# A third mixture of experts computed on its chosen pairs, and rows stationary in the routed first product

## The reference

```python
def _L2_ffn_ref(x, gate_w, fc1_w, fc1_b, geglu_mult, fc2_w, fc2_b, s_fc1_w, ...):
    E, TOPK = (15, 3)                              # F = 256, shared FS = 512
    scores = jax.nn.softmax(xt @ gate_w.T, axis=-1)
    topk_w, topk_idx = jax.lax.top_k(scores, TOPK)
    topk_w = topk_w / (jnp.sum(topk_w, axis=-1, keepdims=True) + 1e-20)
    h = jnp.einsum('td,efd->etf', xt, fc1_w) + fc1_b[:, None, :]
    xh, g = (h[..., :F], h[..., F:])
    a = jax.nn.gelu(g, approximate=False) * xh * geglu_mult[:, None, :]
    yexp = jnp.einsum('etf,edf->etd', a, fc2_w) + fc2_b[:, None, :]
    y = jnp.einsum('etd,te->td', yexp, comb)       # + the shared expert, 512 wide

def _L3_ffn_ref(u, g_shared, W1_s, b1_s, W2_s, b2_s, g_routed, W1_r, b1_r, W2_r, b2_r, centroids):
    E_R, E_S, K = (8, 2, 2)                        # H = 1024
    # shared experts on every token, then per token the K of 8 chosen by sigmoid(u @ centroids)
```

## Time and profile before

| | |
|---|---|
| median of 3 runs | 2613.74 us (2607.96 to 2623.17) |
| profiled execution | 2616.16 us, its span 2614.3 us |
| granted clock of TensorE, mean | 0.886 |
| TensorE busy (matmul) | 2166.2 us, 83% of the span |
| VectorE busy | 1535.2 us, 59% |
| ScalarE busy | 1121.6 us, 43% |
| GpSimd busy | 586.0 us, 22% |
| HBM read and written | 154.11 MB and 18.38 MB |

### The profile page before, as it was taken

How to read it: one execution, slowest core, us unless ns; L and a number is a source line. 1 busy time by engine, 2 the same in 40 slices (tenths; PEclk the granted TensorE clock), 3 DMA queues, 4 the chain that set the end, 5 groups by cost and what they waited for, 6 DMA issues and landing times. The chain is left out here.

```text
span 2614.3 us, 42273 instructions
## 1 busy us (share of the span) xinstructions
PE 2166.2 (83%) x14834; PEld 1685.9 (64%) x14834; DVE 1535.2 (59%) x3631; ACT 1121.6 (43%) x3143; POOL 586.0 (22%) x725
## 2 busy tenths in 40 slices
PE   5799674668999976869978868989996999798893
PEld 3566441226777754559956538879995566598883
DVE  4566648996556553556555554545554556556865
ACT  5566344452444433533311444523332366455652
POOL 0200017992000010010022420000003222213555
PEclk9899787899999986669977979979997899697987
DMA  3000012210000003314310014322210000245762
GB/s 110 9 2 2 33 67 76 64 63 33 1 1 1 1 31 115 111 62 165 116 41 0 5 31 122 92 95 92 92 43 35 5 8 4 92 155 174 228 212 87
DMA packets 58247, 174.92 MB, mean 67 GB/s; under 512 B 18327, under 2 KB 28155, under 8 KB 56008
## 3 DMA queue, kind: packets, MB, share of 16 engines
q1 hardware_dynamic: 56012, 169.23, 20.1%
q0 software_dynamic: 2048, 3.29, 0.4%
HBM read 154.11 MB, written 18.38 MB: 66 GB/s over the span
## 5 line engine op out<-in xcount | busy, mean ns | idle before, releaser
L2410 PE MATMUL ps<-l1a_zc,tables_sb 128*128 128x400 f32 x256 | 108.8, 558 | 95.2 <-POOL l1a_zc L2339 60.3
L2410 PEld LDWEIGHTS ps<-l1a_zc,tables_sb 128*128 128x128 f32 x256 | 47.3, 202 | 156.6 <-POOL l1a_zc L2339 88.3
L1912 ACT ACTIVATE l1x_probs<-ps,l1x_nmax 100x361 f32<-100x361 f32 x128 | 70.7, 558 | 164.5 <-DVE l1x_nmax L1987 164.5
L2350 POOL TENSOR_TENSOR l1a_dbx<-l1a_dx,l1a_rows 128x400 f32<-128x400 f32 x128 | 130.5, 1059 | 7.0 <-DMA l1a_rows<-l1a_rows_spilled 4.9
L2363 ACT ACTIVATE ps<-l1a_delta,weights 128x400 f32<-128x400 f32 x128 | 76.5, 598 | 81.1 <-DVE ps L2393 53.1
L1026 ACT ACTIVATE l3x_probs<-l3x_s_sb,l3x_nmax 100x361 f32<-100x361 f32 x128 | 75.3, 589 | 70.4 <-DVE l3x_nmax L1115 66.4
L1024 ACT ACTIVATE l0x_probs<-ps,l0x_nmax 100x361 f32<-100x361 f32 x128 | 70.7, 557 | 65.0 <-DVE l0x_nmax L1122 56.8
L3024 PE MATMUL ps<-l3f_routed_x_high,l3f_routed_w_low 128*128 128x128 f32 x320 | 95.5, 298 | 3.5 <-DVE l3f_routed_w_low L3088 1.7
L3025 PE MATMUL ps<-l3f_routed_x_high,l3f_routed_w_high 128*128 128x128 f32 x320 | 95.3, 298 | 0.0
L3026 PE MATMUL ps<-l3f_routed_x_low,l3f_routed_w_high 128*128 128x128 f32 x320 | 95.2, 298 | 0.0
L2602 PE MATMUL ps<-l2f_x_high,l2f_w_high 128*128 128x400 f32 x272 | 95.0, 349 | 0.0
(11 more groups left out here) (714 smaller groups left out, 6754.5 us busy)
## 6 DMA issues: line engine op xcount, KB each, us to landing
ctxT<-l_ffn_units SPq DMA_DIRECT2D x20, 1026.0 KB, 5.7
l3f_expert<-l_ffn_units SPq DMA_DIRECT2D x20, 1026.0 KB, 5.5
l2x_a_taps<-l2x_taps_spread SPq DMA_DIRECT2D x8, 1912.5 KB
l2f_landing<-l_ffn_units SPq DMA_DIRECT2D x17, 771.0 KB, 6.0
l1a_rows<-l1a_rows_spilled SPq DMA_DIRECT2D x32, 400.0 KB, 3.5
l1f_gates<-l1f_gates SPq DMA_DIRECT2D x16, 800.0 KB, 4.1
l1f_positions<-l1f_staged SPq DMA_DIRECT2D x16, 621.9 KB
l1f_landing<-l_ffn_units SPq DMA_DIRECT2D x16, 512.0 KB, 3.5
```

The source lines that it names most:

```text
L2350: pool.tensor_tensor(dbx[:, n % BUFS, :], dx[:, j, m, :], rows[:, g % RING, 0, :], ALU.mult).then_inc(s.dbx_ready, 1)
L2410: pe.matmul(y_bank(m), st.ident, zc[:, n % DONE, :], start=(i == 0), stop=(i == NS - 1)).then_inc(s.sum_done, 1)
```

## The change

The third mixture takes the form of the fourth. Its two shared units stay dense, and its 15 experts run on chosen pairs: 3 a token, 33 tiles of 128 rows, one unit a tile (a unit now is the whole expert: 512 first columns, 256 hidden). Only one of the four slots is filled ahead during the shared units, because of memory (`early=1`); the other three are allocated at the start of the routed part.

In the routed part of both mixtures the first product is turned round: the rows (`x_high`, `x_low`) are stationary and the weights move, 512 columns in one matmul. The hidden values then come out with rows on partitions. The bias is one more matmul: a 64-row pick of the tile's expert (`pick`, made on GpSimd from `mine`) against the bias rows, high parts in rows 0 to 31 and low parts in rows 32 to 63. Gelu is one instruction instead of four; TensorE turns the hidden values (`turn_hidden`), and ScalarE and VectorE cut them from PSUM. The second product runs two units behind the first instead of one. The high parts of the first weights are made on ScalarE (`cut_first`) instead of VectorE. Rows have six slots (`ROW_SLOTS`), in `XT`, instead of two. In the tail a batch's power (`rstd_pool`) stands three batches behind its gathers, instead of behind all of them. At the start of the program the first pack is issued ahead of `XT`, the first stage starts without waiting for `X`, and `ctxT` is loaded after it.

```diff
 class Routes:
     SLOTS = 4
...
-        self.landing = [spare[:, i * size:(i + 1) * size].rearrange("p (q c) -> p q c", q=2) for i in range(2)]
-        self.landing += [sb(f"expert{i}", [P, 2, unit_cols])[:] for i in range(2, self.SLOTS)]
+        self.landing = [spare[:, i * q * c:(i + 1) * q * c].rearrange("p (q c) -> p q c", q=q) for i in range(lent)]
+        self.early, self.slot_shape = early, [P, q, c]
+        self.landing += [sb(f"expert{i}", self.slot_shape)[:] for i in range(lent, early)]
...
     def sync_first_loads(self, sp):
-        for u in range(self.SLOTS):
+        for u in range(self.early):
             self.sync_load(sp, u)
...
 def routed_experts(nc, st, routes, kind, bias, gain=None):
...
             @block.sync
             def _(sp):
                 def load_rows(i):
-                    after(sp, s.x_turned, i - 1)
...
+                    after(sp, s.x_turned, i - ROW_SLOTS + 1)
...
+                for u in range(routes.early, R):
+                    routes.sync_load(sp, u)
                 sp.wait_ge(routes.scattered, 16 * B * routes.top)
-                load_rows(0)
-                load_rows(1)
+                for i in range(ROW_SLOTS):
+                    load_rows(i)
                 for u in range(U):
                     if u + R < U:
                         sp.wait_ge(s.w1_split, u + 1)
                         sp.wait_ge(s.w2_split, u + 1)
-                        sp.wait_ge(s.gelu_done, 4 * (u + 1))
+                        if geglu:
+                            sp.wait_ge(s.h_split, u + 1)
                         routes.sync_load(sp, u + R)
...
+                    if u % H == H - 1 and u // H + ROW_SLOTS < N:
+                        load_rows(u // H + ROW_SLOTS)
+                    done = u // H - 1
+                    if u % H == 0 and done >= 0:
+                        sp.wait_ge(s.y_copied, done + 1)
+                        sp.dma_start(routes.results[done * P:(done + 1) * P, :], y_rows[done % 2][:]).then_inc(routes.stored[done % 2], 16)
...
                 def first(u):
...
-                    after(pe, s.gelu_done, 4 * (u - 1))
-                    for j in range(4):
-                        out = h_bank(u, j)
-                        for k in range(KT):
-                            lo, hi = w1(w_low, u, j // 2, k, j % 2), w1(w_high, u, j // 2, k, j % 2)
-                            pe.matmul(out, r(lo), r(x_high[i % 2][:, k, :]), start=(k == 0), stop=False)
-                            pe.matmul(out, r(hi), r(x_high[i % 2][:, k, :]), start=False, stop=False)
-                            last = pe.matmul(out, r(hi), r(x_low[i % 2][:, k, :]), start=False, stop=(k == KT - 1))
...
+                    pe.wait_ge(s.pick_ready, i + 1)
+                    after(pe, s.hidden_done, u - 1)
+                    pe.matmul(h_bank(u), r(pick[i % 2][:]), r(bias_parts[:, h * 512:(h + 1) * 512]), start=True, stop=False)
+                    for k in range(KT):
+                        hi, lo = r(x_high[i % 2][:, k, :]), r(x_low[i % 2][:, k, :])
+                        pe.matmul(h_bank(u), hi, r(w1(w_low, u, k)), start=False, stop=False)
+                        pe.matmul(h_bank(u), hi, r(w1(w_high, u, k)), start=False, stop=False)
+                        last = pe.matmul(h_bank(u), lo, r(w1(w_high, u, k)), start=False, stop=(k == KT - 1))
...
+                def turn_hidden(u):
+                    pe.wait_ge(s.hidden_done, u + 1)
+                    after(pe, s.h_split, u - 1)
+                    for j in range(J):
+                        last = pe.transpose(turned_bank(u)[:, j, :], hidden[u % 2][:, j, :], st.ident)
...
-                for u in range(U):
...
-                    first(u)
-                    if u:
-                        second(u - 1)
-                second(U - 1)
...
+                for u in range(U + 2):
+                    if u < U:
+                        if turns_at(u) is not None:
+                            turn_rows(turns_at(u))
+                        first(u)
+                    if 1 <= u <= U:
+                        turn_hidden(u - 1)
+                    if u >= 2:
+                        second(u - 2)
...
             @block.vector
...
-                for u in range(U):
+                for u in range(U + 3):
                     if u + 1 < U:
                         split_first(u + 1)
...
+                    if u < U and turns_at(u) is not None:
+                        split_rows(turns_at(u))
+                    if u >= 3 and (u - 3) % H == H - 1:
+                        copy_results((u - 3) // H)
+                    if u < U and geglu:
+                        product(u)
+                    if 1 <= u <= U:
+                        split_hidden(u - 1)
...
 def l2_ffn(nc, st, dram):
...
-        experts(nc, st, "l2f", "geglu", E + 2, landing, gate,
-                lambda i, sl: i * 2 + sl, [(0, xf)], st.w["f8b2"])
-        experts_tail(nc, st, "l2f")
+        experts(nc, st, "l2f", "geglu", 2, landing, gate, lambda i, sl: E + sl, [(0, xf)], st.w["f8b2"], routes)
+        routed_experts(nc, st, routes, "geglu", st.w["f8b1"])
+        routed_tail(nc, st, routes)
```

More of the change, by code:

```diff
@@ L2818, with __init__ @@
 ROW_TILES = -(-TOK // P)
+GATHER_LAG = 3
+ROW_SLOTS = 6
 class Routes:
     SLOTS = 4
-    def __init__(self, nc, ctx, st, name, experts, top, units, first_unit, unit_cols, constants, spare):
+    def __init__(self, nc, ctx, st, turn, name, experts, top, units, first_unit, halves, unit_cols, constants, who, source, spare=None, early=SLOTS):
         def sb(n, shape, dt=F32):
@@ L2957, in sb @@
             return ctx.enter_context(nc.sbuf_tensor(f"{name}_routed_{n}", shape, dt))
-        w_high, w_low = [sb(f"w_high{i}", [P, 2, offb]) for i in range(2)], [sb(f"w_low{i}", [P, 2, offb]) for i in range(2)]
-        x_rows = [sb(f"x_rows{i}", [P, D]) for i in range(2)]
+        landing = routes.landing
+        landing += [sb(f"expert{i}", routes.slot_shape)[:] for i in range(routes.early, R)]
+        w_high, w_low = [sb(f"w_high{i}", [P, Q, offb]) for i in range(2)], [sb(f"w_low{i}", [P, Q, offb]) for i in range(2)]
@@ L2964, in routed_experts @@
+        hidden = [sb(f"hidden{i}", [P, J, P]) for i in range(2)]
+        h_high, h_low = [sb(f"h_high{i}", [P, J, P]) for i in range(2)], [sb(f"h_low{i}", [P, J, P]) for i in range(2)]
         y_rows = [sb(f"y_rows{i}", [P, D]) for i in range(2)]
-        sems = ["rows_loaded0", "rows_loaded1", "x_turned", "x_cut", "x_split", "w1_cut", "w1_split", "w2_cut", "w2_split",
-                "h_ready", "gelu_done", "h_cut", "h_split", "second_done", "y_copied"]
+        pick = [sb(f"pick{i}", [64, P]) for i in range(2)]
@@ L2977, in after @@
                     eng.wait_ge(sem, value)
-            def weights_here(eng, u):
-                eng.wait_ge(routes.loaded[u % R], 16 * (u // R + 1))
             @block.sync
@@ new lines, in _ @@
+                cut_first(0)
+                cut_rows(0)
+                for u in range(U + 2):
+                    if u + 1 < U:
+                        cut_first(u + 1)
+                    if u < U:
+                        if turns_at(u) is not None:
+                            cut_rows(turns_at(u))
+                        raise_hidden(u)
+                    if 1 <= u <= U:
+                        cut_hidden(u - 1)
+                    if u < U:
+                        cut_second(u)
@@ L3118, in _ @@
                 for u in range(U):
+                    i = u // H
+                    if u % H == 0:
+                        after(pool, s.h_ready, H * (i - 1))
+                        pool.tensor_copy(r(pick[i % 2][:]), routes.mine[:, i:i + 1].to_broadcast([64, P])).then_inc(s.pick_ready, 1)
                     pool.wait_ge(s.w2_cut, u + 1)
@@ L3131, in routed_tail @@
         y = st.yT[:].rearrange("p m (b t) -> p m b t", b=B)
-        with stage_sems(nc, NORM_SEMS + [f"gathered{j}" for j in range(B)] + ["shares_added"]) as s, nc.Block(no_gpsimd_drain=True) as block:
-            gathered = [s.gathered0, s.gathered1, s.gathered2, s.gathered3, s.gathered4, s.gathered5, s.gathered6, s.gathered7]
+        with stage_sems(nc, NORM_SEMS + ["shares_added"]) as s, nc.Block(no_gpsimd_drain=True) as block:
+            gathered = routes.gathered
             @block.gpsimd
```

222 lines of the change are left out of this document (135 added, 87 removed).

## The result

The changed kernel took 2841.49 us (median of 4 runs, 2829.16 to 2846.57) against 2618.45 for the one before (4 runs): ratio 1.0848, interval 1.0793 to 1.0904. It is 8.5% slower, where 2597 was predicted.

The account below looks back on a forecast made before the run. TensorE bounded the dense third mixture; in the routed fourth it waited for rows, VectorE next. Terms +17, -28.5, -2.6 and -2.5 sum to -16.6, from 2616.2 to 2599.6, or 2597 by the runs' median; range 2560 to 2640.

Parts of the forecast that it names:

- the shared operands: Fourth mixture: cycle over two units through the second weights' cut, GpSimd's and VectorE's splits and both products, 4.28 us a unit.
- SyncE's order: Fourth mixture: result copy wait, store, odd unit's load, cut, split and copy, 8.8 to 9 us for two units, 4.5 each.
- a start term of 2.5: Program start: the first stage no longer waits for the tokens, 800 KB, -2.5 us.
- The first product: Routed parts, TensorE: a 512-column matmul takes 0.23 us, in proportion from 400 columns; seven take 1.6.
- Landings: Weight loads in the routed parts: 771 KB land in 4.55 us (bounds 3.6 and 6.0), 1,026 KB in 5.5.
- Routed start: Third mixture: rows lie behind three loads in one queue; 12 us with expert number, transpose, cut and split.
- Tail: Third mixture: gathers 30.4 us, powers 4.5, then 8; fourth mixture: 4.5 + 8.5 for 15.6, -2.6.
- Scatters: Third mixture: 24 scatters take 37 us, as long as the two shared units, so they cost nothing.
- Rows: Fourth mixture: six row slots remove TensorE's wait for rows, 18.0 us in all.
- The low clock: Rival, both routed parts: TensorE at half clock throughout, +97 us, 2694; chance 0.16.
- loads hidden: Rival: slots come back in time, ScalarE sets the third mixture's pace, shared operands the fourth's; -37 and -16, 2544; chance 0.17.
- landings of 6.0: Rival, third mixture: landing takes 6.0 us, pace 5.4, +19, 2616, no change; chance 0.17.

Follow-up runs that it names:

- the pick ahead: Against the changed kernel, GpSimd casts the next tile's pick ahead of the second weights' split of the current tile's last unit, not behind it: 2589.01 us.
- the stores later: On the pick ahead, SyncE stores each tile's results one tile later in its written order: 2589.89 us.
- filler: Against the changed kernel, TensorE makes 16 unread products of 256 columns ahead of each new tile's first product: 2796.07 us.
- the multipliers copied out: On the stores later, GpSimd copies each geglu unit's two multipliers out of the slot: 2552.03 us in one run, 2567.19 in five more.

## Why the prediction was wrong

**The step that failed** is one sentence on the third mixture: "GpSimd's wait for second weights and its 128-column pick hide under the load." It was carried over to the fourth without a word. It priced the pick by its length, and looked for cover for that. What counts is what stands ahead of it: GpSimd takes its instructions in the written order (the pick starts at 1793.24, as the split ahead of it ends), so the pick comes after a split that needs the second product of two units before. The prediction had a loop through exactly these instructions for the fourth ("the shared operands"), over two units; the pick made it one tile, and in the third, where a tile is a unit, doubled it. The pace was 8.38 and 7.56 instead of 4.82 and 4.69: 33 x 3.56 + 40 x 2.87 = 232 us of the 244.7 by which the profiled executions differ from the sum.

**What the rest was worth.** With the pick ahead the same terms can be compared again. The fourth's pace is 4.69, as predicted; the third's 4.46 for 4.82. From the fourth's routing to the end it is -28.2 for -31.1; the third mixture +6.5 (552.3 for 545.8) for +17, with 12 less by that pace; before it -5.9 for -2.5. The time, 2589 for 2597, lies in the range. Some of this agreement is luck. The 4.69 was worked out from SyncE's order, and with the stores later, which takes that loop away, it stayed at 4.63. And the part up to the selection, whose instructions are the same in the changed kernel and in all experiments, took from 1711.3 to 1721.4 us in their profiles, so that a start term of 2.5 can't be judged. Term by term:

- *The first product.* Starts of two 512-column matmuls, at half clock and at the full one:

```profile
1788.67 0.63 PE L3052 MATMUL ps<-l2f_routed_w_high,l2f_routed_x_high 128*128 128x512 f32 x1
1789.09 0.63 PE L3053 MATMUL ps<-l2f_routed_w_high,l2f_routed_x_low 128*128 128x512 f32 x1
...
2613.75 0.40 PE L3052 MATMUL ps<-l3f_routed_w_high,l3f_routed_x_high 128*128 128x512 f32 x1
2613.99 0.39 PE L3053 MATMUL ps<-l3f_routed_w_high,l3f_routed_x_low 128*128 128x512 f32 x1
```

0.42 and 0.24 us; the 0.23 taken from 400 columns was right.
- *Landings.* In the changed kernel 4.2 for 771 KB (4.55 predicted, 6.0 the upper bound) and 5.4 for 1,026 KB (5.5), as the rows show; with the pick ahead, where the loads follow each other faster, 4.4 and 6.0:

```profile
l3f_expert<-l_ffn_units SPq DMA_DIRECT2D x20, 1026.0 KB, 5.4
l2f_routed_expert<-l_ffn_units SPq DMA_DIRECT2D x24, 771.0 KB, 4.2
```

- *SyncE's order.* "SyncE's other waits in the row end before the hidden split and cost nothing": wrong as a statement on the third mixture (60.3 us of waits for result copies with the pick ahead), harmless in size, since both loops are equally long. In the fourth I had it as the longer loop, 4.5 against 4.28; with the stores later the pace is 4.63 for 4.69, so another was as long there too.
- *Gate.* 12.7 from the selection to the next block (1714.4 to 1727.06), 13.0 predicted. *Routed start:* 12.7 from that block's first ScalarE instruction (1774.69) to the first bias product, 12 predicted. From the last shared matmul it is 15.9, and 15.4 with the pick ahead, just over the 15 that I had named as a sign of being wrong (2.7 + 12 in the sum).
- *Tail.* 35.4 from the first to the last gather, 34.9 predicted with the powers; from there 8.2 to the next stage, 8 predicted.
- *Scatters.* Hidden, but barely: in the changed kernel the last starts at 1760.5 and the last shared matmul at 1771.5; with the pick ahead, where the shared units took 10 us less, it is 1761.8 and 1760.3. The next block's first pick starts 3.4 and 3.1 us behind that matmul.
- *Rows.* TensorE waits for rows once, at the start; but six slots were worth 160 us and not 18, since two would have closed a loop of their own.

**The rivals.** The low clock (0.16) came nearest in time, 2694, and its mark was seen: the clock was 0.67 and 0.77 in the two parts, under the 0.8 that I had named. It isn't the cause: filler gave 40 us, and with the pick ahead the clock came back by itself. The Trainium skill (TensorE: Matmul & The Clock Gate, HAM oscillation) says that every burst begins at the lower clock where it is shorter than the wait behind it. By the forecast's own numbers (2.7 us of work, 2.0 of idleness) that condition wasn't met, so the rule didn't lead to 2694, as the prediction says. Nor does it describe this trace: bursts of some 5.3 us were longer than their waits of 3.1 to 3.6, yet 21 of the 33 in the third mixture began at the half clock (11 began at the full one, and one in between); in the fourth all 20 bursts of a tile began at the half. The low clock adds to a loop which something else closes. Neither loads hidden nor landings of 6.0 came about.

**What stays open.** The two shared units took 44.5 us in the changed kernel's profile (1727.06 to 1771.54) and 34.4 with the pick ahead, with the same instructions; a second profile of the kernel with the multipliers copied out showed 43.9 where the first had 34.5. In the long ones TensorE, VectorE and ScalarE stand idle for stretches in the second unit, and the view has no reason for it: it puts up to 6.8 us of VectorE's waiting down to a transfer of an earlier layer (`l1a_rows`), and 7.4 us to nothing. No experiment was made on it. The sum had 36 to 37 for the two units, so this is 8 of the remaining 12 us. Another 5 lie in the stages between the mixtures, from the first instruction behind the third mixture to the fourth's routing: 299.9 us against 295.0 before, with the same instructions. Over all the profiles that stretch takes 288.0 to 299.9, so differences of 10 us between single profiles mean little unless they lie in the part that was changed.

## What to carry to other kernels

For every small instruction that a change adds, write down what stands ahead of it in its engine's order and what that waits for, not only its length: a cast of 1.28 us cost 237 because it stood one place too late. Where products are in flight two deep, follow one full round from a buffer's use to its next use through each engine's written order, and count how many units the round spans; the pace is its length by that number, and each new wait can lower the number. When taking one wait away gives nothing, look for a second of the same length before concluding that it was free. And compare profiles stretch by stretch: a few us that turn up in a part with the same instructions aren't the edit's.

## What the runs showed of the hardware

A wait view that names the instruction which came last can name one that isn't waited for: 30 waits were put down to the rows' low part, and moving the pick, which ended 0.2 us earlier, took nearly all of them away (2 are left, 0.7 us). The gap gave it away: 0.06 us from the named instruction's end to the product, 0.25 from the pick's. TensorE's clock was at the half for one burst and at the full for the next, each behind 16 filler products and 1.3 us of idleness (bias product 0.76 at 1901.99, 0.47 at 1909.99), so the idle time just ahead of a burst didn't decide it. GpSimd's cast of 64 x 128 values took 0.28 us in some places and 1.28 in others. In the changed kernel all 50 long ones overlap one of VectorE's splits of weights, and the 3 short ones overlap none.
